# Tokenizer of a vision tower: keys on crossed array lanes, values on straight ones, and the output product moved ahead of the second scores

## The reference, cut to what matters

```python
def _L0_tok_ref(features, ...):                      # features: 32, 64, 64, 64
    x = features.reshape(b, c, h, s, w, s)
    reduce_feats = x.mean((3, 5)).reshape(b, c, hw).transpose(0, 2, 1)
    unf = x.transpose(0, 1, 2, 4, 3, 5).reshape(b, c, hw, n).transpose(0, 2, 3, 1)
    q = _ln(reduce_feats, ln_q_w, ln_q_b) @ Wq.T
    kv = _ln(unf, ln_kv_w, ln_kv_b) @ Wkv.T
    attn = softmax(einsum('bhpd,bhpnd->bhpn', q * scale, k), axis=-1)
    aggre = einsum('bhpn,bhpnd->bhpd', attn, v)
    return reduce_feats + aggre @ proj_w.T + proj_b
```

## Time and profile before

| what | value |
|---|---|
| median of three executions | 620.93 us (620.38 to 623.08) |
| span of the profiled execution | 621.0 us |
| PE busy over the span | 579.8 us (93%) |
| DVE busy | 524.2 us (84%) |
| ACT busy | 448.5 us (72%) |
| POOL busy | 447.6 us (72%) |
| granted TensorE clock, mean | 0.981 |

### The profile page before, as it was taken

One profiled execution on the slowest core, in us unless ns is written; L12 is line 12 of the kernel. 1 busy time (PEld: TensorE's weight loads), 2 busy tenths in 40 slices (PEclk: granted clock), 3 DMA queues, 4 the chain that ended last, 5 costly groups with the idle time before them and its releaser, 6 DMA issues. The chain is left out here.

```text
span 621.0 us, 15981 instructions
## 1 busy us (share of the span) xinstructions
PE 579.8 (93%) x5276; PEld 306.2 (49%) x5276; DVE 524.2 (84%) x1029; ACT 448.5 (72%) x936; POOL 447.6 (72%) x458
## 2 busy tenths in 40 slices
PE   7999999999999999999768997999868999999995
PEld 4223333333333333333235664666536888888884
DVE  3599999999999999999765885989988888888883
ACT  4887778777877777786247986888856777777772
POOL 5957988899889889955765153566677767667676
PEclk9999999999999999999889998999998999999999
DMA  7432333332223333000008498111114333322200
GB/s 275 158 141 115 136 137 137 137 122 73 95 121 137 136 137 136 20 1 12 4 0 217 97 166 142 53 36 39 35 53 115 80 86 84 81 71 69 73 21 1
DMA packets 49602, 58.19 MB, mean 94 GB/s; under 512 B 31932, under 2 KB 44836, under 8 KB 47544
## 3 DMA queue, kind: packets, MB, share of 16 engines
q1 hardware_dynamic: 44120, 49.23, 26.3%
q0 software_dynamic: 5120, 6.99, 3.6%
q10 hardware_dynamic: 288, 1.05, 0.4%
HBM read 50.19 MB, written 10.28 MB: 97 GB/s over the span
## 5 line engine op out<-in xcount | busy, mean ns | idle before, releaser
L831 PE MATMUL s_proj<-x_px,w_kv 64*64 64x512 f32 x256 | 130.5, 602 | 0.9 <-DVE qk L607 0.9
L837 PE MATMUL s_proj<-x_px,w_kv 64*64 64x512 f32 x256 | 130.6, 602 | 0.0
L2164 POOL DMA_INDIRECT out<-orow,m_rows x96 | 94.5, 984 | 40.5 <-issue 34.4
L1264 POOL DMA_INDIRECT rows_by_group<-r_pay,r_slot_i x64 | 65.7, 1026 | 47.7 <-ACT r_pay L1406 9.1
L501 POOL TENSOR_TENSOR half_px<-x_px 128x1024 f32<-128x1024 f32 x30 | 71.3, 2377 | 29.8 <-DMA x_px<-in_x 29.8
L522 POOL TENSOR_TENSOR pre<-va 128x1024 f32<-128x1024 f32 x32 | 76.2, 2382 | 21.8 <-DVE va L623 20.0
L607 DVE TENSOR_TENSOR qk<-s_proj,q 128x512 f32<-128x512 f32 x128 | 85.4, 678 | 5.0 <-PE s_proj L837 2.8
L623 DVE TENSOR_TENSOR va<-b_a,v_sb 128x1024 f32<-128x1024 f32 x62 | 75.6, 1219 | 7.5 <-PE b_a L875 7.5
L317 ACT ACTIVATE x_sq<-x_px 128x1024 f32<-128x1024 f32 x64 | 67.2, 1050 | 18.6 <-PE b_x L912 18.6
L2133 PE MATMUL s_delta<-m_xsT,m_w_cur 128*64 128x128 f32 x1152 | 71.1, 273 | 0.0
L831 PEld LDWEIGHTS s_proj<-x_px,w_kv 64*64 64x64 f32 x256 | 31.5, 134 | 74.0 <-issue 52.3
(11 more groups left out here) (318 smaller groups left out, 1746.8 us busy)
## 6 DMA issues: line engine op xcount, KB each, us to landing
x_px<-in_x SPq DMA_DIRECT2D x15, 2048.0 KB, 7.6
m_rows<-rows_by_group SPq DMA_DIRECT2D x96, 72.0 KB
wt<-in_w2T SPq DMA_DIRECT2D x8, 512.0 KB
rows_by_group<-rows_by_group SPq DMA_DIRECT2D x1, 2286.0 KB, 9.6
out<-orow,m_rows POOLq DMA_INDIRECT x96, 2.3
x_px<-in_x ACTq DMA_DIRECT2D x2, 512.0 KB, 5.9
x_px<-in_x SPq DMA_DIRECT2D x2, 512.0 KB, 7.1
rows_by_group<-r_pay,r_slot_i POOLq DMA_INDIRECT x64
```

What stands on the lines that cost most here:

```text
L831: mm(b_k[i][LO, :], w_kv[LO, 0, :], px(t, j, LO), start=True, stop=True)
L837: mm(b_k[i][HI, :], w_kv[HI, 0, :], px(t, j, HI), start=True, stop=True).then_inc(done["kv_product"], 1)
L1264: g.indirect_dma_start(rows_d, bass.IndirectOffsetOnAxis(ap=slot_i[:, c % 2, k:k + 1], axis=0), pay[:, c % 2, k, :], None).then_inc(scatte ...
L2164: nc.gpsimd.indirect_dma_start(out_d, bass.IndirectOffsetOnAxis(ap=rows[:, i, ID0:ID0 + 1].bitcast(I32), axis=0), orow[:, i, :], None, bou ...
```

## The change

In `kv`, keys go to the crossed lanes and values to the straight ones, so the keys of the two images lie on swapped partition halves. `q_mm` goes to the crossed lanes likewise, since the query must lie as the keys do. To match it, `q_rstd` and `pool_bias` on ACT are written across the halves, as two instructions of 64 partitions each in place of one of 128. `h1` holds the images swapped from there on; `out_mm` keeps its lanes, and the routing's token numbers (an iota on POOL) get the swap. The masks of the moments are swapped.

The values that are split are now those of chunk 0: the first half in `kv(t, 0)`, the second (`values_behind`) after the second scores, beside `q_mm`. `out_mm` moves, for tiles 0 to 12, from behind the last `spread` to ahead of the second scores, and writes the second half of the bank `b_x`; it waits for `q_var` in place of `kv_mean_sq`. `pre4` has two buffers. `finish` on DVE moves one iteration on, to ahead of `scores_max`, and `qk_mul(t-1, 0)` moves ahead of `shift_scores`. `mean` now waits for `finish` where `square_sum` did. `copy_v(t, 0)` waits for `first_values`.

```diff
             act.wait_ge(done["q_ln"], t + 1)
-            a.activation(rq[:, :], rq[:, :], ACT.Exp, scale=-0.5).then_inc(done["q_rstd"], 1)
+            for h, across in ((LO, HI), (HI, LO)):
+                a.activation(rq_across[across, :], rq[h, :], ACT.Exp, scale=-0.5).then_inc(done["q_rstd"], 1)
...
-            act.wait_ge(done["kv_product"], NCH * t + n + 1)
+            if n == 0:
+                act.wait_ge(done["first_values"], t + 1)
+            else:
+                act.wait_ge(done["kv_product"], NCH * t + n + 1)
...
             q_scale(t - 1)
+            if t - 5 <= LAST_EARLY:
+                finish(t - 5)
             scores_max(t - 2)
             va_mul(t - 3, 2)
+            qk_mul(t - 1, 0)
             shift_scores(t - 2)
-            qk_mul(t - 1, 0)
             qk_mul(t - 1, 1)
             sum_exps(t - 2)
             qk_mul(t - 1, 2)
             scale_exps(t - 2)
-            if t < TILES + 2:
+            if LAST_EARLY < t - 4 < TILES - 2:
                 finish(t - 4)
...
-            mm(b_k[i][LO, :], w_kv[LO, 0, :], px(t, j, LO), start=True, stop=True)
...
+            mm(b_k[i][HI, :], w_kv[LO, 0, :], px(t, j, LO), start=True, stop=True)
+            cols = FIRST if n == 0 else slice(0, CH)
+            mm(b_v[i][LO, cols], w_kv[LO, 1, :], px(t, j, LO)[:, cols], start=True, stop=True)
+            mm(b_v[i][HI, cols], w_kv[HI, 1, :], px(t, j, HI)[:, cols], start=True, stop=True)
+            mm(b_k[i][LO, :], w_kv[HI, 0, :], px(t, j, HI), start=True, stop=True).then_inc(done["kv_product"], 1)
...
-            mm(b_x[LO, 0:TOK], gq[LO, :], rs2[LO, 0:TOK], start=True, stop=True)
-            mm(b_x[HI, 0:TOK], gq[HI, :], rs2[HI, 0:TOK], start=True, stop=True).then_inc(done["q_product"], 1)
+            mm(b_x[HI, 0:TOK], gq[LO, :], rs2[LO, 0:TOK], start=True, stop=True)
+            mm(b_x[LO, 0:TOK], gq[HI, :], rs2[HI, 0:TOK], start=True, stop=True).then_inc(done["q_product"], 1)
...
-            values_ahead(t - 1)
             mean(t - 1)
...
-            if t != TILES + 2:
+            if t > LAST_EARLY + 4 and t != TILES + 2:
                 out_mm(t - 4)
...
             if t > 0:
                 kv(t, 0)
+            if t <= LAST_EARLY + 4:
+                out_mm(t - 4)
             scores(t - 1, 1)
+            if t > 0:
+                values_behind(t)
             q_mm(t)
```

More of the change, by code:

```diff
@@ L140, in tokenizer @@
         "q_scaled q_ready squared moments square_sums kv_mean_sq kv_var kv_clamped kv_ln kv_rstd kv_product v_copied "
-        "qk_ready scores scores_scaled scores_max scores_shifted exps exp_sum exp_recip exps_scaled weights "
+        "qk_ready first_values scores scores_scaled scores_max scores_shifted exps exp_sum exp_recip exps_scaled weights "
         "a_spread va_ready halved quartered paired folded attn_out h1_ready")
@@ L335, in pool_bias @@
                 act.wait_ge(folded, FOLDED)
-            a.activation(h1[:, TOK * t:TOK * t + TOK], rs2[:, 0:TOK], ACT.Identity, scale=1.0 / NP, bias=vec[:, 7:8]).then_inc(done["pooled_biased"], 1)
+            for h, across in ((LO, HI), (HI, LO)):
+                a.activation(h1[across, TOK * t:TOK * t + TOK], rs2[h, 0:TOK], ACT.Identity, scale=1.0 / NP, bias=vec[h, 7:8]).then_inc(done["pooled_biased"], 1)
         def q_mean(t):
@@ L705, in q_scale @@
                 return
-            v.wait_ge(done["q_rstd"], t + 1)
+            v.wait_ge(done["q_rstd"], 2 * t + 2)
             v.wait_ge(done["q_product"], t + 1)
@@ L830, in kv, with values_behind @@
                 pe.wait_ge(done["v_copied"], m - 1)
-            mm(b_k[i][LO, :], w_kv[LO, 0, :], px(t, j, LO), start=True, stop=True)
[L832 to L845, removed]
+            mm(b_k[i][HI, :], w_kv[LO, 0, :], px(t, j, LO), start=True, stop=True)
[3 more added lines that the diff above has]
+            mm(b_k[i][LO, :], w_kv[HI, 0, :], px(t, j, HI), start=True, stop=True).then_inc(done["kv_product"], 1)
+        def values_behind(t):
             if not live(t):
                 return
[L849 to L853, removed]
+            j = ORDER[0]
+            mm(b_v[0][LO, SECOND], w_kv[LO, 1, :], px(t, j, LO)[:, SECOND], start=True, stop=True)
+            mm(b_v[0][HI, SECOND], w_kv[HI, 1, :], px(t, j, HI)[:, SECOND], start=True, stop=True).then_inc(done["first_values"], 1)
         def spread(t, i):
@@ L894, in mean @@
             pe.wait_ge(done["q_scaled"], t + 1)
+            if t > 3:
+                pe.wait_ge(done["h1_ready"], t - 3)
             if t == 0:
@@ L939, in out_mm @@
             pe.wait_ge(done["folded"], t + 1)
-            if t + 3 < TILES:
-                pe.wait_ge(done["kv_mean_sq"], t + 4)
+            if t < LAST_EARLY:
+                pe.wait_ge(done["q_var"], t + 5)
             else:
                 pe.wait_ge(done["kv_var"], TILES)
+            if t > LAST_EARLY:
                 pe.wait_ge(done["h1_ready"], t)
-            mm(b_x[LO, 0:TOK], w_ld[HI, 3, :], pre4[HI, :], start=True, stop=True)
-            mm(b_x[HI, 0:TOK], w_ld[LO, 3, :], pre4[LO, :], start=True, stop=True).then_inc(done["attn_out"], 1)
+            mm(b_x[LO, TOK:2 * TOK], w_ld[HI, 3, :], pre4[HI, t % 2, :], start=True, stop=True)
+            mm(b_x[HI, TOK:2 * TOK], w_ld[LO, 3, :], pre4[LO, t % 2, :], start=True, stop=True).then_inc(done["attn_out"], 1)
         def centre_first(i):
@@ L1228, in path_weights @@
             u = lambda k: pay[:, q, :, P0 + 6 + k]
-            done(g.iota(pay[:, q, :, ID0:ID0 + 1].bitcast(I32), pattern=[[P, QC], [0, 1]], base=P * QC * c, channel_multiplier=1))
+            done(g.iota(pay[:, q, :, ID0:ID0 + 1].rearrange("p (k b f) o -> p k b (f o)", k=2, b=2).bitcast(I32), pattern=[[4 * P, 2], [-2 * P, 2], [P, 2]],
+                        base=P * QC * c + 2 * P, channel_multiplier=1))
             done(g.tensor_tensor(u(1), pw[:, q, :, 0], bits[:, q, 5, :], ALU.mult))
```

26 lines of the change are left out of this document (14 added, 12 removed).

## The result

| | before | after |
|---|---|---|
| median (14 executions each) | 620.97 us (619.84 to 625.03) | 618.51 us (614.32 to 620.28) |
| ratio of times, with its 95% interval | | 0.9939 (0.9917 to 0.9961) |
| span of the profiled execution | 621.0 us | 615.4 us |
| second scores of the last tile | 294.66 us | 291.70 us |

The change makes the kernel faster by 0.61% (0.39 to 0.83), that is 3.8 us (2.4 to 5.2); the two medians lie 2.5 apart. The forecast was 4.5 us and 616.5, the range 613.0 to 619.0.

The account below looks back on a forecast made before the run. A loop of DVE's softmax chain and PE's work behind it was taken to bound the kernel. Terms -4.13 - 0.62 - 0.43 + 0.2 + 0.5 = -4.5 took 621.0 to 616.5 us; range 613.0 to 619.0.

Parts of the forecast that it names:

- the loop that was named: Second scores to end of `weigh` on DVE, a signal, then PE to the next second scores: 17.52 us a period.
- The two rivals with other mechanisms: PE binding without DVE's chain, 613.0 to 613.8 (chance 0.13); waiting matmuls stopping other lanes, 627 (chance 0.06).
- PE alone: Rival: DVE's chain stays at or below 10.40, every period is 17.28, time 613.0 to 613.8; chance 0.13.
- Lanes do not block: Denies the rival that keys in `kv` cannot overtake waiting values, the loop growing by 0.48 to 627; chance 0.06.
- iteration 1: No softmax chain exists there yet: put at 0, bounds 0 and 0.43 gained.
- iteration 2: Exponential 0.66 later behind the product of chunk 0, less 0.43 from the lanes: a loss taken as 0.2.
- iteration 3: PE binds without DVE's `finish`; the lanes gain 0.43.
- iterations 4 and 5: Iteration 4 has no `finish` and gains 0.62 with PE binding; iteration 5 gains the regular 0.375.
- iteration 16: Output product of tile 12 ahead of the scores and its `finish` in the chain: a loss of 0 to 0.76, taken at 0.5.
- the new period: DVE's chain 10.64, signal 0.14, PE's part 6.74: 17.52 us, gaining 0.375 a tile over eleven periods.
- halves of a unit: Lane count from moments to second scores: a unit is 0.86 us, the stretch loses half a unit, 0.43.
- The gain is eaten: Rival: DVE's softmax chain delayed behind `q_final` and a less covered exponential, 618 to 620.5; chance 0.21.

Follow-up runs that it names:

- first experiment: The changed kernel with the last `va_mul` of a tile moved behind `weigh`: median 614.5 us, 0.9890 of before.
- the kernel of the four edits: The changed kernel with last `va_mul` behind `weigh`, `q_mm` ahead of `values_behind`, old DVE order in iteration 2, `copy_v(t-1, 1)` ahead of the exponential: 613.21 us.

## Why the prediction was right, and where its sum was off

**The mechanism.** The time fell, within the range, and by the loop that was named: a chain on DVE and PE's work behind it, with the first scores right behind `weigh` and not behind the square sums. The two rivals with other mechanisms fell. PE alone does not bind in a regular period of the kernel after (a wait of 0.27 ahead of the first scores), and the scores follow the square sums without a wait as soon as the chain is shortened (first experiment). In iteration 4, which the prediction gave to PE alone at 17.28, the kernel after takes 17.29 (63.68 to 80.97). Lanes do not block: L845 at 148.33 starts ahead of L843 at 149.17, which comes before it in the program. By the Trainium skill's rule in "TensorE: Matmul & The Clock Gate", Part 3, quoted in the prediction, it should not; the trace of this kernel says as that of before did that a waiting matmul on one lane does not stop a later one on another.

**The sum.** Forecast -4.5 up to the end of the tokenizer; the traces have -2.96 (294.66 to 291.70). By its terms, from the second scores in the table and in the fences, and for iteration 5 before:

```profile
99.50 1.07 PE L887 MATMUL b_s<-qk,sel 128*32 128x512 f32 x8
```

In us, forecast and measured as differences to before:

| stretch | forecast | measured | how |
|---|---|---|---|
| iteration 1 | 0 | +0.16 | 29.70 to 29.86 |
| iteration 2 | +0.2 | +0.26 | 16.31 to 16.57 |
| iteration 3 | -0.43 | -0.45 | 17.70 to 17.25 |
| iterations 4 and 5 | -1.00 | -0.87 | 35.79 to 34.92 |
| iterations 6 to 15 | -3.75 | -2.57 | 178.95 to 176.38 |
| iteration 16 | +0.5 | +0.51 | 16.21 to 16.72 |

The term that was mis-sized is the new period, "10.64 + 0.14 + 6.74 = 17.52": it is 17.63, and ten of them make most of the 1.2 us between the fifth row's numbers. Parts of a few hundredths add up: 0.05 in the chain, 0.05 in PE's part, 0.01 in the signal. In the chain, `q_scale` waits 0.06 for the query product, which is issued behind the values; the run with the query product ahead takes that away and the period falls by just that. In PE's part, the crossed lanes run 0.06 behind the straight ones at the second scores, so the stretch shortens by 0.38 and not 0.43, and the part is 6.79. The signal is 0.15 for 0.14. Against a gain of 0.375 a tile a tenth is a quarter, and the working by halves of a unit had no room for it. The rest of the fifth row is one longer period, 17.75 in iteration 10 (169.10 to 186.85): there `finish` starts 0.45 after `q_scale` (170.91 to 171.36), elsewhere 0.34 (153.28 to 153.62). Five of the six other kernels with `finish` right behind `q_scale` show the same in the same iteration (the one with the step of two SBUF inputs does not), and what holds it there stays open. Iteration 1 is not the change's doing as far as these runs show: over the eight kernels in the table that start from the change its second scores come between 29.65 and 29.95.

The part of the chain that was worked out link by link held. The exponential waits for `shift_scores` as forecast (`shift_scores` 4.81 after the second scores; forecast 4.75), and DVE stands 0.14 for it ahead of `sum_exps` (157.54 where its pace of 0.60 would have it, 157.68 where it starts; forecast 0.15).

**The gain is eaten.** This rival was partly true. It priced 0.2 us of delay a tile at 618.7; the period has 0.11, so by the traces 618.0 was left (620.97 less 2.96), at the edge of its 618 to 620.5. The delay was not where the rival had it, behind `q_final` and the exponential, but at the query product and at the crossed lanes' end. Iteration 2 alone shows the wait for `q_final`.

So the width of the range did some of the work. The forecast's own range was 615.2 to 617.8. The median of 618.51 lies outside it, in the nearer part of this rival's range, which the prediction had taken in; the ratio of times, 0.9939, puts the time at 617.2, inside it. By the medians, 2.5 us apart, the change falls among those that the prediction could not tell from no change (chance 0.22), by the ratio, 3.8 us, among the faster ones (0.72).

**Span and time.** The prediction said that nothing lies between the span of 621.0 and the median of 620.93. In each execution that was timed the time is about 1.8 us above its span (after: 617.18 and 615.4). So the profiled execution of before stands for a time near 622.8, longer than ten of its fourteen, and that of after, 617.18, is shorter than its median of 618.51; part of the 5.6 us between the spans is that. The windows from the last second scores to the end, before ...

```profile
294.66:621.00 326.34, 290.54 (x2742) 209.00 (x2738) 267.02 (x621) 226.43 (x564) 205.42 (x272) 0.96 0.31 72
```

... and after:

```profile
291.70:615.40 323.70, 289.79 (x2740) 208.41 (x2738) 267.18 (x622) 225.46 (x563) 203.99 (x272) 0.96 0.31 73
```

The same work takes 2.64 us less there. But the kernel of the four edits, whose tokenizer ends 5 us sooner still, takes 325.3 for it, and the nine kernels of the table take from 323.1 to 326.3, with the same scan, routing and trees in the eight changed ones. So these 2.64 us are within what this part varies by, and are not counted as the change's. Over the fourteen executions of the kernel after, the span goes with the mean granted clock: 612.5 to 613.1 us in the three at 0.984 or more, 617.2 to 618.5 in the five at 0.976 or less. In the trace of after the clock is 1.00 in the period shown above and less in parts of the scan:

```profile
300.00:320.00 20.00, 13.66 (x70) 5.81 (x72) 14.08 (x22) 5.60 (x11) 15.17 (x14) 0.80 0.00 0
320.00:340.00 20.00, 18.55 (x88) 10.64 (x89) 9.58 (x15) 15.16 (x32) 10.44 (x25) 0.85 0.70 180
```

With means of 0.80 and 0.85, part of each stretch is at the lower of the two levels, 1.2 GHz; PE had 6 us without work in the first of them. Whether the clock makes the difference between executions, or goes with something else that makes it, stays open. What can be said is that the change is worth 3.0 us in the tokenizer by the traces, which is within the 2.4 to 5.2 by the times; whether it is above or below 0.5%, 3.1 us, neither tells.

## What to carry to other kernels

Read PE by lanes before you call it full: 93% busy stood before and after, and half a unit per tile lay in it. When a stretch of one engine is shortened in a loop over two, work out the other's chain step by step, waits for signals and for issue order included, for once that chain binds, as here, a tenth of a microsecond in it is a tenth in the period; then look for a step in the chain that nobody on it needs, as the last `va_mul` was here. An order that pays in the steady state may cost in the first iterations, where another engine is early or late; these can have an order of their own.

## What the runs showed of the hardware that was not expected

An addition of 128x256 on DVE takes 0.41 us with one input from PSUM, and took 2.38 and 1.61 with both inputs from SBUF while POOL worked on a 128x1024 tile; it ended 0.28 after POOL's instruction both times. The kernel with it took 27 us more than the one with an input from PSUM (648.6 and 621.42). The Trainium skill says in "SBUF — State Buffer", section "SBUF: two separate sides", that such a DVE operation and a GpSimd operation that reads SBUF take turns on a port pair and that the later one is blocked for the whole of the other. These two rows agree. In a kernel like this one, with POOL busy on SBUF, an added DVE step wants one input in PSUM.

A matmul on a lane of its own started within 0.02 us of its neighbours (152.47 to 152.49), but its place in the order of issue still counted: 0.06 us for the query product behind two others.
